# Attention over keys: the causal bias opens the score accumulation, and ScalarE runs a slot's exponential ahead of the older slot's second turned half

## The reference

```python
# sublayer 4: causal self-attention with ALiBi, 16 heads of 8 features
att = jnp.einsum('bqhd,bkhd->bhqk', q, k) * scale / temperature
bias = slopes[:, None, None] * rel[None, :, :]
bias = jnp.where(causal[None, :, :], bias, -jnp.inf)
w = jax.nn.softmax(att + bias[None, :, :, :], axis=-1)
y = jnp.einsum('bhqk,bkhd->bqhd', w, v)          # then W_proj, residual, layer norm
# sublayer 5: cross-attention to ctx_1024, 16 heads of 8 features
scores = jnp.where(m == 0, -1e9, scores)         # m is the mask over keys
out = jnp.einsum('bhqk,bkhd->bhqd', jax.nn.softmax(scores, axis=-1), v)
```

## Time and profile before

| | us |
|---|---|
| median of 3 runs (lowest, highest) | 1607.38 (1606.27, 1607.75) |
| span of the profiled execution | 1613.9 |
| PE busy in it | 1328.9 |
| DVE busy | 1207.8 |
| ACT busy | 1069.4 |
| first to last L350 of this stage (128 of them) | 946.2 to 1516.5 |

### The profile page before, as it was taken

The page is one execution under the profiler, slowest core; times in us unless marked ns, Lnnn a source line. Parts: engine busy times, 40 slices in busy tenths (PEclk is TensorE's granted clock), DMA queues, the critical chain, the costliest instruction groups (busy, mean ns, idle before and its releaser), DMA issues.

```text
span 1613.9 us, 63504 instructions
## 1 busy us (share of the span) xinstructions
PE 1328.9 (82%) x26438; PEld 858.1 (53%) x26438; DVE 1207.8 (75%) x2613; ACT 1069.4 (66%) x2260; POOL 762.8 (47%) x1558
## 2 busy tenths in 40 slices
PE   5787888888885777777767779999999899989897
PEld 2454555555554444444333346666666666666685
DVE  2445655655544888888799969998999999999856
ACT  2465576766654788887666767777777777777645
POOL 2334344545444677777788843333333232323133
PEclk8789899999987899997575679999999999999979
DMA  7000000000000000000000000000000000000012
GB/s 195 8 2 3 2 3 3 3 3 3 3 2 15 16 23 17 23 17 16 1 1 1 1 2 3 3 3 3 3 3 9 23 16 16 17 23 9 3 40 66
DMA packets 28670, 24.27 MB, mean 15 GB/s; under 512 B 3676, under 2 KB 23906, under 8 KB 28386
## 3 DMA queue, kind: packets, MB, share of 16 engines
q1 hardware_dynamic: 28386, 20.21, 4.6%
HBM read 15.94 MB, written 4.19 MB: 12 GB/s over the span
## 4 chain that ended last, share of the span: by engine, by line
PE 31%; issue 25%; POOL 22%; ACT 15%; DVE 7%; SPq 0%; DMA 0%; POOLq 0%; ACTq 0%; DVEq 0%
PE keys_T L589 7%; ACT keys_pexp L674 5%; POOL gla_low L1155 4%; PE keys_E L485 3%; POOL cross_pairs L836 3%; ACT xs L317 3%; POOL gla_yg L1179 3%; ACT keys_pT L656 2%; POOL cross_spread L803 2%; PE keys_E L528 2%; POOL gla_sq L1172 2%; PE keys_O L596 2%; DVE ffn_hh L1988 1%; PE keys_S L331 1%; ACT keys_vz L647 1%
## 5 line engine op out<-in xcount | busy, mean ns | idle before, releaser
L656 ACT ACTIVATE keys_pT<-keys_T 128x512 f32<-128x512 f32 x256 | 152.5, 596 | 107.2 <-PE keys_T L589 103.9
L340 POOL TENSOR_SCALAR keys_spread<-keys_kT,keys_heads 128x512 f32<-128x512 f32 x128 | 86.9, 698 | 259.2 <-ACT keys_kT L620 259.2
L350 DVE TENSOR_REDUCE keys_mx<-keys_S 128x16 f32<-128x1024 f32 x128 | 156.5, 1223 | 37.3 <-PE keys_S L555 22.4
L589 PE MATMUL keys_T<-ident_sb,keys_pexp 128*128 128x128 f32 x1024 | 165.1, 284 | 22.5 <-ACT keys_pexp L674 18.5
L589 PEld LDWEIGHTS keys_T<-ident_sb,keys_pexp 128*128 128x128 f32 x1024 | 112.9, 141 | 98.5 <-ACT keys_pexp L674 50.5
L353 DVE TENSOR_TENSOR keys_pe_in<-keys_S,keys_mx 128x1024 f32<-128x1024 f32 x128 | 156.7, 1225 | 4.4
L1611 DVE COPY_PREDICATED gla_at<-gla_node,gla_GP 128x256 f32<-128x256 int32 x128 | 64.8, 506 | 101.9 <-ACT gla_at L1468 98.4
L674 ACT ACTIVATE keys_pexp<-keys_pe_in 128x1024 f32<-128x1024 f32 x128 | 134.1, 1048 | 0.0
L709 DVE RECIPROCAL keys_rinv<-keys_O 128x128 f32<-128x128 f32 x128 | 120.4, 941 | 0.0
L1155 POOL TENSOR_TENSOR gla_low<-gla_ex,gla_kT 128x128 f32<-128x128 f32 x160 | 71.9, 480 | 80.1 <-ACT gla_ex L1459 80.1
L1172 POOL TENSOR_TENSOR gla_sq<-gla_o 128x512 f32<-128x512 f32 x32 | 33.2, 1039 | 150.9 <-ACT gla_o L1476 150.9
(11 more groups left out here) (285 smaller groups left out, 3719.9 us busy)
## 6 DMA issues: line engine op xcount, KB each, us to landing
context<-in_ctx_T SPq DMA_DIRECT2D x32, 256.0 KB, 2.7
xs<-in_x SPq DMA_DIRECT2D x8, 512.0 KB, 7.3
out_x<-xs SPq DMA_DIRECT2D x16, 256.0 KB, 2.3
keys_mask_q<-keys_mask_b SPq DMA_DIRECT2D x64, 1.0 KB
keys_bias_right_f<-in_alibi_right SPq DMA_DIRECT2D x1, 512.0 KB, 3.8
ffn_w<-in_L_ffn_w_gate_T SPq DMA_DIRECT2D x1, 256.0 KB, 4.7
ffn_w<-in_L_ffn_w_up_T SPq DMA_DIRECT2D x1, 256.0 KB, 4.9
ffn_w<-in_L_ffn_w_down_T SPq DMA_DIRECT2D x1, 256.0 KB, 5.9
```

The source lines that it names most:

```text
L340: nc.gpsimd.tensor_scalar(spread[:, :, :, j, :].rearrange("q t s k -> q (t s) k"), flat.rearrange("q (a k) -> q a k", k=SEQ), heads[:, j:j ...
L350: nc.vector.tensor_reduce(m, quads(S), X, ALU.max).then_inc(c["mx"], 1)
L589: last = nc.tensor.transpose(T[:, j * P:(j + 1) * P], pexp[:, t % 2, (4 * half + j) * P:(4 * half + j + 1) * P], sh.ident[:, :])
L656: nc.scalar.activation(pT[:, t % 2, 4 * half:4 * half + 4, :].rearrange("q n k -> q (n k)"), T[:, :], ACT.Copy).then_inc(c["pT"], 1)
```

## The change

Two edits in `attention_over_keys`. On PE, the four causal bias matmuls go ahead of the eight score matmuls and carry the flag that starts the accumulation; the scores then add to it and the last of them signals `scores`. The masked half keeps its order. On ACT, in `second`, the exponential of tile n goes ahead of take1 of tile n-1 and of the norm. Operations, operands, counts and waits are otherwise the same.

```diff
                 c.free_last(pe, "sub", g, t, 1)
-                tensor_scores(nc, S, qT[:, p, t * TILE:(t + 1) * TILE], spread[:, p, t, :, :, :], stop=False)
+                if not masked:
+                    for r in range(4):
+                        nc.tensor.matmul(S[:, r * 512:r * 512 + QH * SEQ], bias_left[:, :],
+                                         bias_right[:, r * QH * SEQ:(r + 1) * QH * SEQ], start=True, stop=False)
+                last = tensor_scores(nc, S, qT[:, p, t * TILE:(t + 1) * TILE], spread[:, p, t, :, :, :],
+                                     start=masked, stop=not masked)
...
-                else:
-                    for r in range(4):
-                        last = nc.tensor.matmul(S[:, r * 512:r * 512 + QH * SEQ], bias_left[:, :],
-                                                bias_right[:, r * QH * SEQ:(r + 1) * QH * SEQ], start=False, stop=True)
                 last.then_inc(c["scores"], 1)
...
             def second(g, p, t):
-                if n := back(g, p, t, 1, 2 * NG):
-                    take(*n, 1)
-                if n := back(g, p, t, 7, 2 * NG):
-                    scalar_normalise(nc, act, sh, b, c, *n)
                 if n := back(g, p, t, 0, 2 * NG):
                     gg, _, tt = n
...
                     nc.scalar.activation(pexp[:, tt % 2, :], pe_in[:, tt % 2, :], ACT.Exp).then_inc(c["exp"], 1)
+                if n := back(g, p, t, 1, 2 * NG):
+                    take(*n, 1)
+                if n := back(g, p, t, 7, 2 * NG):
+                    scalar_normalise(nc, act, sh, b, c, *n)
```

## The result

The changed kernel takes 1685.71 us (median of 4 runs, 1679.5 to 1687.8), beside 1607.16 us for the kernel before. The ratio is 1.048, with a 95% interval of 1.0433 to 1.0528: slower by some 79 us.

A forecast was written before the change was run, and what follows sets the result against it. The ScalarE loop through the exponential bounds masked slots and causal q, PE alone causal k and x. Loop growth 73.8, bias edit 0 and clock 5 sum to 79 us slower: median near 1686, range 1662 to 1714.

The forecast's parts named there:

- The new loop: Attention stage: W, T0, O, e, e copy, exp, take1, W again; 20.34 us per causal group, 20.15 masked.
- The old loop: Attention stage before: T0, O, e, T1, take1, norm, exp, without W; in every masked slot and the causal q slot.
- no net change: Rival, attention stage: W enters, norm and T1 leave, loops equally long; time 1607, chance 0.03.
- No slack of take1 before W: Attention stage: W already waits for take1, so take1's 0.95 us delay by one exponential passes on to W.
- the faster rival: Between take1 and W: take1's delay does not hold W, so DVE (masked) and PE (causal) bind; 1568, chance 0.07.
- the estimate of 0.14: 64 causal slots on PE: one array-shape change fewer saves about 0.14 us a slot if scores are on the path; 0 taken.
- the 5 us taken for the clock: PE in the attention stage: less dense work may lower its clock; a third of the masked half's 16 us price.
- The 2.8 and 4.0 us of idle PE per group: Attention stage: PE idle after T1, S and the wait for W, per causal and masked group, beyond today's idle time.
- the high end of the range: Whole kernel: 1714 us, from a 19 us error on the slot sums plus up to 16 us for the clock.

The follow-up runs named there:

- W-last run: W moved on PE from ahead of T0 to behind T1, against the changed kernel; 1602.34 us, ratio 0.9993 to the kernel before.

## Why the prediction was right

*The new loop.* As said, W, T0, O, e, e copy, exp, take1, and W again; the chain above is that list. Group sums: 20.34 predicted and 20.48 measured in the causal half, 20.15 and 20.30 in the masked half. By slot, the causal x, k and q are within 0.02 us of their sums; v has all of the rest, 5.99 against 5.85. There the exponential and take1 do not overlap, as they do in the other slots: after the two v copies, exp starts only when they have ended and take1 only when exp has ended. I had given the exponential 0.95 us everywhere.

*The old loop* was read less well. The prediction lists it as T0, O, e, T1, take1, norm, exp, and says that the change takes T1 out of it. In the masked half of the kernel before that is so in the x slot alone, where take1 starts when T1 has ended:

```profile
1403.80 0.44 PE keys_E L506 x4
...
1404.27 0.67 PE keys_T L589 x4
...
1404.96 0.03 ACT keys_pT L656
```

In the k, q and v slots take1 comes right behind the e copy, and the chain does not pass T1 (1400.46 to 1400.95, 1408.71 to 1409.30). So the e copy was in the loop before as well, and the argument against "no net change", that it now comes in, does not hold for these slots. What did change there is that W came in, at about 1.0 us, and the norm left, at about 0.4: the masked q slot grew from 4.33 us (exponential to exponential, 1405.94 to 1410.27 in the chain of before) to 4.98 (W to W, 1449.59 to 1454.57 after). The sum does not suffer by it, because it adds up the new loop whole and takes the old one's length as measured.

*No slack of take1 before W*, the point that decided against the faster rival: W waits for it in 51 of some 51 masked slots. The W-last run shows that this wait carries the loss: without it the changed order costs nothing.

*Bias edit.* Hidden in the changed kernel, as said: the exponential edit alone gives 1684.55 and both give 1685.71. Alone it gives 0.11 us in a slot that the chain passes on PE; the estimate of 0.14 had the right sign and size. The Trainium skill (TensorEngine Tiling (Array Packing), Key Properties) says that a change of tiling mode drains TensorE. The run with the bias edit alone agrees, one change fewer per slot going with 0.11 us less, and the time is saved behind T1, where the change fell away; but no run changes the shape and nothing else.

*The clock.* Windows of 25 us of the changed kernel in the masked half (columns of the earlier trace rows):

```profile
1250.00:1275.00 25.00, 20.19 (x437) 14.35 (x439) 20.44 (x31) 16.72 (x27) 5.93 (x15) 1.00 0.04 13
1275.00:1300.00 25.00, 20.58 (x431) 14.30 (x427) 18.70 (x28) 14.14 (x25) 5.42 (x14) 0.93 0.05 13
1370.00:1395.00 25.00, 19.55 (x444) 14.13 (x444) 19.53 (x28) 15.03 (x25) 7.62 (x21) 0.93 0.04 13
1535.00:1560.00 25.00, 19.83 (x442) 14.70 (x444) 19.41 (x28) 14.60 (x25) 6.89 (x18) 0.93 0.05 14
```

The granted clock is 1.00 in most of the stage, and falls to 1.2 GHz for a short time in three places, here as means of 0.93; each follows a v slot's wait of W for take1, 1.69 us long, and PE was busy for about 20 of 25 us in these stretches. The kernel before had no such fall between 975 and 1500 us. Over the stage, 32 groups at the measured periods are 652.5 us for 128 slots, or 647.4 for the 127 between first and last reduce; 651.2 were measured. So clock and start together cost under 4 us. Before, the same reckoning leaves 0.7. The clock by itself can be read from the three groups with a fall: from reduce to reduce they take 21.91, 21.89 and 21.83 us where their neighbours take 20.30, so 4.7 us in all, and the 5 us taken for the clock was about right.

*The sum agrees better than its terms.* The median rose by 78.6 us, where 79 was forecast. But the stage has grown by 80.9 us (570.3 to 651.2, just above the 640 to 650 that the prediction names), and the span only by 72.1, to 1686.0, where a span near 1692 was forecast. The last stage gave some back. Its window in the kernel before:

```profile
1516.00:1613.90 97.90, 82.88 (x744) 68.75 (x728) 57.34 (x258) 49.73 (x128) 30.59 (x81) 0.86 0.16 44
```

and in the changed kernel, from the same point in the program:

```profile
1595.40:1686.00 90.60, 75.30 (x741) 62.59 (x728) 57.31 (x258) 48.93 (x127) 30.55 (x81) 0.94 0.17 48
```

It is 7.3 us shorter, with a mean clock of 0.94 in place of 0.86, and its instructions are the same. The profiled execution of before was itself 6.5 us above the median of its runs; it had about 20 us at 1.2 GHz early in that stage, and the changed one's fall there was shorter. With the bias edit alone or W last this stage kept more of its clock too, and runs of the kernel before spread from 1594.47 to 1613.68 us in a later session. What decides how long that fall lasts was not tried and stays open. That the forecast of 1686 for the median came out to the microsecond is luck by a few us: the v slots were put 4.6 us too low in all, and the time outside the stage changed too.

*Slips in the working.* The 2.8 and 4.0 us of idle PE per group that the prediction calls "beyond the idle time of today" are all of its idle time (20.34 - 17.57 and 20.15 - 16.11); 0.5 and 1.7 us of it were there before. And the high end of the range, by its own terms, is 1607 + 74 + 19 + 16 = 1716, not 1714. Neither changes the forecast.

## What to carry to other kernels

Where engines hand work round in a ring, write out the loop and ask of each instruction whether it is in it: an early start for one instruction is a late start for those it passes, and what counts is which of them somebody waits for. Here the exponential was early enough and take1 was not; the cheap and useful move was the norm, the one instruction that nobody needs soon (31 us gained), not the exponential past take1 (79 lost). To price a position, double a harmless instruction there: 44 us in the loop, 0 outside it.

## What the runs showed of the hardware

Behind four full-array transposes (T1) the score matmuls on 32-row pieces start 0.59 us after the transposes do, and the full-array bias matmuls 0.49 us after them (the causal x slot, before and with the bias edit alone); a change of array shape fewer goes with about 0.1 us less. The time between the starts of an exponential of 1024 elements and the copy behind it is 0.95 us in most slots and 1.08 us in the slot with the two 64-row copies ahead (1150.28 to 1151.36 in the changed kernel's timeline of ACT); I have no cause for the difference. PE's granted clock fell to 1.2 GHz in three of the 16 masked groups of the changed kernel, each time after a wait of 1.69 us in the v slot, and cost about 1.6 us each time; in the other groups the same slot brought no fall.
